# A two-layer vision tower on one core: seven token tiles as split float32r products, ternary weights made on ScalarE, narrower bias products, an epsilon folded into the norm's aggregation, and new instruction orders

## Chip, cores and metric

The kernel runs on one core of one Trainium2 chip. The metric is the device time of one execution in microseconds, as the median of three runs.

## What is computed

The input is 32 images of 3x96x96. They are cut into 36 patches each, so there are 32 x 37 = 1184 tokens of width 256, the first of each image being a class token.

```python
h = tok(x)                            # patches (1152 x 768) @ W.T (768 x 256) + b, class token, + pos_enc
h = h + attn0(_layernorm(h), ...)     # second layernorm, z = sigmoid(n @ Wg.T + bg), c = n @ Wc.T + bc, a scan
                                      # h = (1 - z) h + z c over the tokens of an image, plus its own input
h = h + ffn0(_layernorm(h), ...)      # gelu(x @ absmean(W_fc).T), layernorm(1024) * ln_w + ln_b, @ absmean(W_proj).T
h = h + attn1(_layernorm(h), ...)     # rope, causal softmax attention inside an image, output projection
h = h + ffn1(_layernorm(h), ...)      # round(x / scale) clipped to +-127, @ (ternary - 1).T, + bias

def _absmean_core(W):                 # the ternary weights of ffn0
    gamma = jnp.mean(jnp.abs(W)) + EPS
    Ws = W / gamma
    Wq = jnp.sign(Ws) * jnp.minimum(jnp.round(jnp.abs(Ws)), 1.0)
```

## The kernel before

The 1152 patch rows are 9 tiles of 128. The class tokens are the same for all images up to the attention, so they are carried as one column beside the tiles (stages `c_...`). Each engine has its own program, written out by hand as a string in `ORDER`: `tok:3` is stage `tok` on tile 3, and an engine runs its stages strictly in that order. Semaphores join the engines.

Stages of a tile: **tok** (PE, L661: six products of 128x128 by 128x256 in plain float32, then one for position and bias at L666), copied out of PSUM by ScalarE (`h0`, L925); statistics on VectorE (`stats`, L1093, and `mean`, L1101, a `bn_aggr`); the power -1/2 on GpSimd (`power`, L1540, after `scaled`, L1535, has added epsilon; `shift`, L1544, makes the bias of the normalisation); `n0` normalises (VectorE); **t0** turns the tile on PE (L673); ScalarE writes the high part and VectorE the low part (`low_part`, L1106), since the gate products are sums of three float32r products (hi hi, hi lo, lo hi; `split_product`, L537). **gate** runs over chunks of three tiles, four blocks each, and is read by two sigmoids on ScalarE (L979, L981) and by VectorE's `gate` (L1360); then **scan** (L1382) and `h1`. After that come `n1`, `t1`, `fc`, gelu, `square`, `gw` (L1414), `high` (L1021), `low`, two DMA transposes, `proj`, then `n2`, `t2`, `qk`, `value`, `rope`, `score`, `attend`, and at last `n3`, `t3`, `out`.

PSUM: `NARROW` gives two banks in turn to everything that is listed for it (`tok`, `c_sum`, `c_square`, `h1`, `proj` and others), `WIDE` three banks to `gate`, `fc` and `qk`. A stage that claims a bank waits until the reader of the bank's last owner is done (`drained`). For `tok:2` that is ScalarE's `h0:1`, for `tok:5` it is `h0:3`.

The ternary weights are made by VectorE in two steps for each of two matrices of 128x2048: `w_below` (L1208) and `w_ternary` (L1214), after ScalarE's sums of absolute values (L886, L891). The bias of `ln_b` through `W_proj` is `w_ln_bias`: 16 products of 128x256 in float16 with a broadcast weight. All loads are issued by SyncE in one queue: x tile 0, the two halves of `w_tok`, small tables, x 1 and 2, `w_gate`, x 3 and 4, `w_fc`, `w_out`, x 5 and 6, `w_pj`, x 7 and 8, then the rest.

## Time and profile before

| | us |
|---|---|
| median of 3 runs | 160.49 |
| lowest, highest | 160.1, 162.58 |
| the profiled execution: its time | 159.69 |
| the profiled execution: span of its instructions | 157.9 |
| share of the span busy: PE, VectorE, ScalarE, GpSimd | 89%, 80%, 61%, 55% |
[...]

The span is 1.8 us shorter than the time of the same execution. All stretches below are given in us from the start of the span. PE is TensorE's matmul, PEld its weight load, DVE VectorE, ACT ScalarE, POOL GpSimd, SPq the queue of SyncE.

### The profile page before, as it was taken

Reading aid. Unit: us, or ns where it says so; the run is one execution under the profiler, and the core shown is the slowest. Engines: PE = TensorE matmul, PEld = TensorE weight load, DVE = VectorE, ACT = ScalarE, POOL = GpSimd, SP = SyncE. Lnnn points to the kernel's source line nnn. Section 1 sums busy time; section 2 is a strip of 40 time slices with the busy share of each in tenths; the row PEclk is TensorE's granted clock in tenths of the full one; section 3 lists DMA queues with packets and bytes.
Section 4 is the critical chain, followed back from the end, with each engine's and each line's share of the span. In section 5 each row is a group of like instructions: output and inputs, shape, how many; then the busy total and the mean of one; then the engine's idle time right before and its main releaser. Section 6 shows DMA issues by size and latency. Waiting matters only on the chain.

```text
span 157.9 us, 3087 instructions
## 1 busy us (share of the span) xinstructions
PE 139.8 (89%) x874; PEld 111.3 (71%) x874; DVE 126.4 (80%) x404; ACT 96.0 (61%) x232; POOL 87.2 (55%) x159
## 2 busy tenths in 40 slices
...
GB/s 163 258 398 425 421 391 238 2 0 0 124 46 0 2 2 2 18 119 133 125 111 104 162 113 108 147 106 149 60 55 0 4 0 0 2 4 0 65 144 103
DMA packets 25621, 17.00 MB, mean 108 GB/s; under 512 B 20069, under 2 KB 23173, under 8 KB 25349
## 3 DMA queue, kind: packets, MB, share of 16 engines
q1 hardware_dynamic: 25605, 16.81, 40.3%
...
HBM read 9.70 MB, written 1.21 MB: 69 GB/s over the span
## 4 chain that ended last, share of the span: by engine, by line
DVE 26%; PE 22%; POOL 21%; issue 11%; ACT 8%; DMA 6%; SPq 4%; DVEq 0%; POOLq 0%; ACTq 0%
POOL small L1540 8%; DMA w_out_int<-w_out_in 6%; PE bank L661 5%; SPq L463 4%; POOL keys L1619 4%; POOL small L1535 4%; PE bank L758 3%; DVE stats L1093 3%; DVE gw L1414 3%; DVE gl L1106 2%; PE bank L832 2%; PE bank L792 2%; DVE rope L1460 2%; POOL small L1544 2%; POOL residual L1592 2%
## 5 line engine op out<-in xcount | busy, mean ns | idle before, releaser
L1540 POOL TENSOR_TENSOR small<-small,powers 128x1 f32<-128x1 f32 (+4 forms) x48 | 39.7, 826 | 6.0 <-DVE small L1403 2.8
L661 PE MATMUL bank<-w_tok,x_raw 128*128 128x256 f32 x108 | 27.7, 411 | 5.8 <-DMA w_tok<-w_tok_in 5.6
L661 PEld LDWEIGHTS bank<-w_tok,x_raw 128*128 128x128 f32 x108 | 21.5, 206 | 8.8 <-issue 5.6
L1535 POOL TENSOR_SCALAR small<-small 128x1 f32<-128x1 f32 x36 | 9.4, 260 | 24.9 <-DVE small L1101 23.2
L537 PE MATMUL bank<-pj,gt_hi 128*128 128x256 f16 x72 | 16.2, 273 | 0.7 <-issue 0.7
L537 PE MATMUL bank<-pj,gt_lo 128*128 128x256 f16 x72 | 16.2, 273 | 0.0
L932 ACT ACTIVATE n<-residual,small 128x256 f32<-128x256 f32 x18 | 10.7, 595 | 9.0 <-POOL small L1544 9.0
L537 PE MATMUL bank<-fc,n1t_hi 128*128 128x512 f16 x36 | 13.6, 379 | 0.6 <-ACT g L1002 0.3
L537 PE MATMUL bank<-fc,n1t_lo 128*128 128x512 f16 x36 | 13.6, 379 | 0.0
L1460 DVE SCALAR_TENSOR_TENSOR rope<-bank,packed,consts 128x324 f32<-128x324 f32 (+2 forms) x24 | 13.1, 608 | 0.3 <-POOL query L1613 0.2
L932 ACT ACTIVATE s<-end,small 108x256 f32<-108x256 f32 (+2 forms) x12 | 7.2, 596 | 9.4 <-POOL small L1544 6.2
L673 PE MATMUL bank<-consts,n 128*128 128x128 f32 x54 | 10.5, 281 | 2.6 <-ACT n L932 2.5
L925 ACT ACTIVATE h<-bank 128x256 f32<-128x256 f32 x9 | 3.4, 381 | 15.0 <-PE bank L666 14.9
L1544 POOL TENSOR_SCALAR small<-small 128x1 f32<-128x1 f32 (+3 forms) x30 | 10.5, 351 | 3.0
L1106 DVE TENSOR_TENSOR gl<-gw,gh 128x1024 f16<-128x1024 f32 x9 | 11.0, 1222 | 1.3 <-ACT gh L1021 1.2
L1562 POOL TENSOR_TENSOR cls<-cls,powers 128x1 f32<-128x1 f32 (+1 forms) x4 | 3.3, 832 | 15.7 <-DVE cls L1256 14.8
L1414 DVE SCALAR_TENSOR_TENSOR gw<-g,small,ln_w 128x1024 f32<-128x1024 f32 x9 | 11.5, 1276 | 0.0
L1002 ACT ACTIVATE g<-bank 128x512 f32<-128x512 f32 x18 | 10.6, 590 | 0.2 <-PE bank L537 0.2
L1021 ACT ACTIVATE gh<-gw 128x1024 f16<-128x1024 f32 x9 | 9.5, 1050 | 1.6 <-DVE gw L1414 1.6
L673 PEld LDWEIGHTS bank<-consts,n 128*128 128x128 f32 x54 | 6.7, 144 | 5.3 <-ACT n L932 3.8
L1012 ACT ACTIVATE squares<-g,small 128x1024 f16<-128x1024 f32 x9 | 10.3, 1146 | 0.0
L537 PE MATMUL bank<-n2t_hi,wq_hi 128*128 128x326 f32 (+2 forms) x24 | 9.1, 378 | 0.0
...
## 6 DMA issues: line engine op xcount, KB each, us to landing
...
w_gate<-w_gate_in SPq DMA_DIRECT2D x1, 512.0 KB, 7.3
w_qk<-w_qk_in SPq DMA_DIRECT2D x1, 512.0 KB, 12.5
ln_w<-ln_w_in SPq DMA_DIRECT2D x1, 512.0 KB, 3.6
```

The source lines that it names most:

```text
L537: last = mm(out, a, b, start=(n == 0), stop=(n == len(pairs) - 1))
L661: mm(out[:, 0:D], x_raw[:, i, k, :], w_tok[:, k, :], start=(k == 0), stop=False)
L673: last = nc.tensor.transpose(out[:, k * 128:(k + 1) * 128], rows_tile[:, k * 128:(k + 1) * 128], ident)
L932: return go(out, h[0:n, i, :], ACT.Identity, scale=small[0:n, i, factor:factor + 1], bias=small[0:n, i, shift:shift + 1])
L1002: go(g[:, i % 2, h * 512:(h + 1) * 512], banks[WIDE[("fc", u)][0]][:, :], ACT.Gelu, accum_out=small[:, i, GS + h:GS + h + 1]).then_inc(s[" ...
L1012: go(squares[:, :], g[:, i % 2, :], ACT.Square, bias=small[:, i, MVG:MVG + 1], scale=-1.0, accum_out=small[:, i, GQ:GQ + 1]).then_inc(s["s ...
L1106: tt(out, full, hi, ALU.subtract).then_inc(ready, 1)
L1414: stt(out=gw[:, i % 2, :], in0=g[:, i % 2, :], scalar=col(i, MVG), in1=ln_w[:, :], op0=ALU.subtract, op1=ALU.mult).then_inc(s["gw_ready"], 1)
L1460: last = stt(out=rope[:, t, 0:width].rearrange("p (m t) -> p m t", t=PATCHES), in0=banks[WIDE[("qk", 4 * c + b)][0]][:, first:first + widt ...
L1535: return nc.gpsimd.tensor_scalar(small[0:n, i, out:out + 1], small[0:n, i, value:value + 1], factor, add, ALU.mult, ALU.add)
L1540: return gt(small[0:n, i, r:r + width], small[0:n, i, ve:ve + width], powers[0:n, 0:width], ALU.pow)
L1544: nc.gpsimd.tensor_scalar(small[0:n, i, nb:nb + 1], small[0:n, i, mv:mv + 1], small[0:n, i, r:r + 1], -1.0, ALU.mult, ALU.mult).then_inc(s ...
```

## The change

Five things are changed together.

1. `tok:2` to `tok:8` use split products: `x_hi` (a rounded copy, ScalarE) and `x_lo` (the rest, VectorE, written over `x_raw`), and likewise `wt_hi` and `wt_lo` once for the weights. Each of the six products of a tile becomes three in float32r. `tok:0` and `tok:1` stay plain. `x_hi` has three slots, which lie in the memory of `hs`, so `scan:0` waits for all of `tok`.
2. The ternary weights: ScalarE scales by 1/gamma and adds a large constant that rounds (`w_round`), then takes the sign (`w_sign`). VectorE's `w_below` and `w_ternary` go.
3. `w_ln_bias` becomes `w_ln_col` (the 16 products with `pj` as weights and 2 columns), a reduction on VectorE, and 2 plain products of 128 columns against the identity that spread the column. `c_sum` of 0, 1 and 3 uses one product where it used two, since `c_h0`, `c_h1` and `c_h2` now also write their sum.
4. Norms 1 and 2: the statistics tile has a third group of count 0 whose sum of squares is 256 epsilon, so that the aggregation gives variance plus epsilon, and GpSimd's `scaled` goes there (18 instructions).
5. `ORDER` is new on all four engines.

The diff, cut (orders down to the part with `gate` and `scan`; declarations, semaphore lists and the same edits in `proj` left out):

```diff
     "tensor": """
-        tok:0 c_sum:0 tok:1 w_gate:0 c_square:0 w_gate:1 tok:2 tok:3 w_gate:2 w_gate:3 tok:4 w_ternary:0 t0:0 t0:1
-        tok:5 t0:2 tok:6 t0:3 tok:7 t0:4 gate:0 gate:1 gate:2 t0:5 tok:8 w_value_bias:0 gate:3 w_ln_bias:0 t0:6 t0:7
-        gate:4 h1:0 h1:1 gate:5 h1:2 t0:8 gate:6 gate:7 w_fold:0 gate:8 w_fold:1 c_sum:1 t1:0 gate:9 h1:3 h1:4
...
+        tok:0 c_sum:0 tok:1 w_gate:0 c_square:0 tok:2 tok:3 tok:4 w_gate:1 w_gate:2 tok:5 t0:0 w_ternary:0 t0:1
+        w_gate:3 tok:6 t0:2 tok:7 t0:3 gate:0 t0:4 w_value_bias:0 gate:1 t0:5 gate:2 tok:8 gate:3 w_ln_col:0 t0:6
+        t0:7 w_ln_bias:0 gate:4 gate:5 h1:0 h1:1 gate:6 t0:8 h1:2 w_fold:0 w_fold:1 gate:7 c_sum:1 gate:8 t1:0
...
     "scalar": """
-        w_sel:0 h0:0 h0:1 w_gate:0 h0:2 c_t0:0 w_abs_fc:0 h0:3 w_abs_pj:0 w_abs_ln:0 h0:4 n0:0 n0:1 t0:0 t0:1 n0:2
-        h0:5 t0:2 h0:6 w_ln_b:0 w_qk:0 t0:3 h0:7 t0:4 n0:3 n0:4 gate:0 n0:5 gate:1 h0:8 t0:5 t0:6 t0:7 w_ln_w:0
-        gate:2 t0:8 gate:3 n0:6 w_fold:0 n0:7 n1:0 w_fold:1 t1:0 n1:1 gate:4 gate:5 n1:2 t1:1 fc:0 n1:3 n0:8 t1:2
...
+        w_tok:0 w_sel:0 h0:0 split:2 w_gate:0 split:3 split:4 h0:1 w_abs_fc:0 h0:2 c_t0:0 h0:3 split:5 split:6 h0:4
+        w_abs_pj:0 w_abs_ln:0 split:7 h0:5 split:8 t0:0 w_round:0 t0:1 h0:6 t0:2 w_qk:0 w_sign:0 h0:7 t0:3 w_ln_b:0
+        w_round:1 gate:0 t0:4 w_sign:1 h0:8 t0:5 gate:1 t0:6 n0:0 n0:1 n0:2 t0:7 gate:2 gate:3 t0:8 n0:3 w_fold:0
+        n0:4 n1:0 n0:5 w_fold:1 w_ln_w:0 n1:1 gate:4 t1:0 n0:6 n1:2 gate:5 t1:1 fc:0 fc:1 n0:7 t1:2 fc:2 fc:3 n1:3
...
     "vector": """
-        c_h0:0 w_ones:0 w_pos:0 c_mean:0 c_var:0 w_small:0 stats0:0 mean0:0 stats0:1 stats0:2 c_norm:0 mean0:1
-        c_lo0:0 n0:0 mean0:2 n0:1 w_gate:0 stats0:3 mean0:3 w_gate_bias:0 stats0:4 w_cut:0 n0:2 w_below:0 w_ln:0
-        t0:0 t0:1 n0:3 mean0:4 w_ln_scale:0 stats0:5 w_ternary:0 n0:4 mean0:5 stats0:6 t0:2 w_below:1 n0:5 w_ln_b:0
-        w_qk:0 mean0:6 t0:3 t0:4 w_ternary:1 stats0:7 gate:0 n0:6 scan:0 mean0:7 t0:5 w_value_bias:0 stats0:8 gate:1
-        n0:7 mean0:8 scan:1 w_ln_bias:0 t0:6 n0:8 h1:0 h1:1 t0:7 stats1:0 stats1:1 h1:2 mean1:0 c_h1:0 t0:8 gate:2
...
+        w_ones:0 w_pos:0 c_h0:0 w_tok:0 c_mean:0 stats0:0 split:2 split:3 stats0:1 c_var:0 split:4 mean0:0 mean0:1
+        c_norm:0 w_gate:0 stats0:2 n0:0 stats0:3 n0:1 split:5 mean0:2 w_small:0 stats0:4 split:6 mean0:3 w_cut:0
+        c_lo0:0 stats0:5 n0:2 split:7 w_ln:0 t0:0 split:8 mean0:4 mean0:5 stats0:6 t0:1 t0:2 n0:3 n0:4 w_ln_scale:0
+        w_gate_bias:0 w_qk:0 mean0:6 t0:3 stats0:7 n0:5 mean0:7 n0:6 w_value_bias:0 w_ln_b:0 gate:0 n0:7 scan:0 t0:4
+        stats0:8 w_ln_col:0 mean0:8 t0:5 gate:1 w_ln_bias:0 scan:1 n0:8 t0:6 h1:0 t0:7 h1:1 stats1:0 c_h1:0 stats1:1
+        h1:2 mean1:0 stats1:2 mean1:1 gate:2 w_fold:0 mean1:2 t0:8 scan:2 gate:3 w_fold:1 scan:3 t1:0 c_mean:1
...
     "gpsimd": """
-        w_tok:0 c_pow:0 h0:0 h0:1 h0:2 h0:3 w_ln:0 h0:4 h0:5 h0:6 h0:7 h0:8 h1:0 h1:1 hc:0 hc:1 h1:2 h1:3 hc:2
...
+        w_tok:0 h0:0 c_pow:0 h0:1 h0:2 h0:3 w_ln:0 h0:4 h0:5 h0:6 h0:7 h0:8 h1:0 h1:1 hc:0 h1:2 hc:1 c_pow:1 hc:2
...
+    x_lo = m.at("x_lo", [TILES, KX, TILE], F32R, x_at)
+    x_hi = m.at("x_hi", [X_SLOTS, KX, TILE], F32R, b_at + both)
...
+            def w_ln_col(_i):
+                out = claim(NARROW, ("ln_col", 0))
                 pe.wait_ge(s["pj_ready"], 1)
                 pe.wait_ge(s["ln_b_hi_ready"], 1)
                 pe.wait_ge(s["ln_b_lo_ready"], 1)
-                split_product(out[:, 0:D], [
-                    (part[:, k:k + 1].to_broadcast([128, 128]), pj[:, k, :])
-                    for k in range(KH) for part in (ln_b_hi, ln_b_lo)
-                ]).then_inc(s["pe_ln_bias"], 1)
+                for b in range(KD):
+                    last = split_product(out[:, 2 * b:2 * b + 2], [
+                        (pj[:, k, b * 128:(b + 1) * 128], ln_b_both[:, k, :]) for k in range(KH)])
+                last.then_inc(s["pe_ln_bias"], 1)
+
+            def w_ln_bias(_i):
+                out = claim(NARROW, ("ln_bias", 0))
+                pe.wait_ge(s["ln_bias_ready"], 1)
+                pe.wait_ge(s["dma_consts"], 32)
+                for k in range(KD):
+                    last = mm(out[:, k * 128:(k + 1) * 128],
+                              derived[:, D_LN_COL + k:D_LN_COL + k + 1].to_broadcast([128, 128]), ident,
+                              start=True, stop=True)
+                last.then_inc(s["pe_ln_bias"], 1)
...
-                    columns = range(C_SOURCE[n], C_SOURCE[n] + KD)
-                split_product(out[:, 0:1], [(ones[:, :], cls[:, c:c + 1]) for c in columns])\
+                    column = C_HSUM + n
+                mm(out[:, 0:1], ones[:, :], cls[:, column:column + 1], start=True, stop=True)\
...
             def tok(i):
                 out = claim(NARROW, ("tok", i))
-                pe.wait_ge(dma_x[i], 16)
-                for k in range(KX):
-                    if i == 0 and k % (KX // 2) == 0:
-                        pe.wait_ge(s["dma_w_tok_b" if k else "dma_w_tok"], 16)
-                    mm(out[:, 0:D], x_raw[:, i, k, :], w_tok[:, k, :], start=(k == 0), stop=False)
+                if i < PLAIN:
+                    pe.wait_ge(dma_x[i], 16)
+                    for k in range(KX):
+                        if i == 0 and k % (KX // 2) == 0:
+                            pe.wait_ge(s["dma_w_tok_b" if k else "dma_w_tok"], 16)
+                        mm(out[:, 0:D], x_raw[:, i, k, :], w_tok[:, k, :], start=(k == 0), stop=False)
+                else:
+                    if i == PLAIN:
+                        pe.wait_ge(s["x_hi_ready"], 1)
+                        pe.wait_ge(s["x_lo_ready"], 1)
+                    pe.wait_ge(s["x_hi_ready"], i - PLAIN + 2)
+                    pe.wait_ge(s["x_lo_ready"], i - PLAIN + 2)
+                    for k in range(KX):
+                        hi, lo = x_hi[:, i % X_SLOTS, k, :], x_lo[:, i, k, :]
+                        mm(out[:, 0:D], hi, wt_hi[:, k, :], start=(k == 0), stop=False)
+                        mm(out[:, 0:D], hi, wt_lo[:, k, :], start=False, stop=False)
+                        mm(out[:, 0:D], lo, wt_hi[:, k, :], start=False, stop=False)
...
+            def w_round(n):
+
+                _, w, _ = ternary[n]
+                act.wait_ge(s["cut_ready"], 2)
+                act.wait_ge(s["round_ready"], 2)
+                go(w[:, :, :], w[:, :, :], ACT.Identity, scale=derived[:, D_INV_GAMMA + n:D_INV_GAMMA + n + 1],
+                   bias=derived[:, D_ROUND:D_ROUND + 1]).then_inc(s["rounded_ready"], 1)
+
+            def w_sign(n):
+                out, w, ready = ternary[n]
+                act.wait_ge(s["rounded_ready"], n + 1)
+                go(out[:, :, :], w[:, :, :], ACT.Sign, bias=derived[:, D_ROUND + 1:D_ROUND + 2]).then_inc(s[ready], 1)
...
+            def w_tok_(_i):
+                act.wait_ge(s["dma_w_tok"], 16)
+                act.wait_ge(s["dma_w_tok_b"], 16)
+                go(wt_hi[:, :, :], w_tok[:, :, :], ACT.Copy).then_inc(s["x_hi_ready"], 1)
+
+            def split(i):
+                act.wait_ge(dma_x[i], 16)
+                if i - PLAIN >= X_SLOTS:
+                    act.wait_ge(s["pe_tok"], i - X_SLOTS + 1)
+                go(x_hi[:, i % X_SLOTS, :, :], x_raw[:, i, :, :], ACT.Copy).then_inc(s["x_hi_ready"], 1)
...
                     dve.wait_ge(s[f"stats{norm}_ready"], i + 1)
-                    nc.vector.bn_aggr(col(i, normed[norm][2], 2, n), stats[0:n, norm, i % 2, 0:6])\
+                    if norm in WITH_EPS and i == 0:
+                        dve.wait_ge(s["powers_ready"], 3)
+                    width = 9 if norm in WITH_EPS else 6
+                    nc.vector.bn_aggr(col(i, normed[norm][2], 2, n), stats[0:n, norm, i % 2, 0:width])\
                         .then_inc(s[f"mv{norm}_ready"], 1)
...
+            def w_tok_(_i):
+                dve.wait_ge(s["x_hi_ready"], 1)
+                low_part(wt_lo[:, :, :], w_tok[:, :, :], wt_hi[:, :, :].bitcast(F32), s["x_lo_ready"])
+
+            def split(i):
+                dve.wait_ge(s["x_hi_ready"], i - PLAIN + 2)
+                low_part(x_lo[:, i, :, :], x_raw[:, i, :, :], x_hi[:, i % X_SLOTS, :, :].bitcast(F32), s["x_lo_ready"])
...
-                for sign, c in ((0.5, D_CUT), (-0.5, D_NEG_CUT)):
-                    ts(derived[:, c:c + 2], total, sign / (HID * D), sign * ABS_EPS, ALU.mult, ALU.add)\
-                        .then_inc(s["cut_ready"], 1)
-
-            ternary = ((fc, w_fc, "fc_ready"), (pj, w_pj, "pj_ready"))
-
-            def w_below(n):
-                out, w, _ = ternary[n]
-                dve.wait_ge(s["cut_ready"], 2)
-                ts(out[:, :, :], w[:, :, :], derived[:, D_NEG_CUT + n:D_NEG_CUT + n + 1], None, ALU.is_lt)\
-                    .then_inc(s["below_ready"], 1)
-
-            def w_ternary(n):
-                out, w, ready = ternary[n]
-                dve.wait_ge(s["below_ready"], n + 1)
-                stt(out=out[:, :, :], in0=w[:, :, :], scalar=derived[:, D_CUT + n:D_CUT + n + 1], in1=out[:, :, :],
-                    op0=ALU.is_gt, op1=ALU.subtract).then_inc(s[ready], 1)
+                ts(derived[:, D_GAMMA:D_GAMMA + 2], total, 1.0 / (HID * D), ABS_EPS, ALU.mult, ALU.add)\
+                    .then_inc(s["cut_ready"], 1)
+                dve.wait_ge(s["cut_ready"], 1)
+                nc.vector.reciprocal(derived[:, D_INV_GAMMA:D_INV_GAMMA + 2], derived[:, D_GAMMA:D_GAMMA + 2])\
+                    .then_inc(s["cut_ready"], 1)
+
+            def w_ln_col(_i):
+                dve.wait_ge(s["pe_ln_bias"], 1)
+                nc.vector.tensor_reduce(derived[:, D_LN_COL:D_LN_COL + KD],
+                                        narrow(("ln_col", 0), 128, 2 * KD).rearrange("p (b t) -> p b t", t=2),
+                                        mybir.AxisListType.X, ALU.add).then_inc(s["ln_bias_ready"], 1)
...
+                if n == 0:
+                    dve.wait_ge(s["pe_tok"], TILES)
...
+                nc.gpsimd.memset(stats[:, 1:3, :, 6:8], 0.0).then_inc(s["powers_ready"], 1)
+                nc.gpsimd.memset(stats[:, 1:3, :, 8:9], LN_EPS * D).then_inc(s["powers_ready"], 1)
...
             def h1_(i):
                 pool.wait_ge(s["mv1_ready"], i + 1)
-                scaled(i, VE1, MV1 + 1, 1.0, LN_EPS).then_inc(s["ve1_ready"], 1)
-                pool.wait_ge(s["ve1_ready"], i + 1)
-                power(i, VE1, R1).then_inc(s["r1_ready"], 1)
+                power(i, MV1 + 1, R1).then_inc(s["r1_ready"], 1)
```

## Rows read from the trace of the kernel before

**Rows 1.** Busy time by stretch: from:to, length, engines' busy us (instructions), clock, DMA.
```profile
10.00:20.00 10.00, 9.87 (x52) 8.77 (x51) 3.15 (x17) 2.37 (x5) 1.08 (x3) 1.00 1.03 422
20.00:34.00 14.00, 13.85 (x77) 12.26 (x75) 12.64 (x47) 9.39 (x22) 7.35 (x18) 1.00 0.45 170
...
47.00:62.00 15.00, 14.42 (x85) 11.78 (x83) 14.18 (x46) 11.22 (x25) 8.35 (x18) 1.00 0.01 2
62.00:80.00 18.00, 15.08 (x119) 9.54 (x120) 17.56 (x52) 17.59 (x42) 13.22 (x19) 1.00 0.55 96
93.00:109.00 16.00, 14.31 (x109) 12.28 (x107) 14.77 (x35) 10.58 (x23) 14.43 (x21) 1.00 0.72 127
```

**Rows 2.** Timeline of PE: start us, us; two plain token tiles.
```profile
25.64 2.76 PE L661 MATMUL bank<-w_tok,x_raw 128*128 128x256 f32 x12
28.05 0.47 PE L666 MATMUL bank<-pos,sel 128*128 128x256 f32 x1
```

**Rows 3.** Timeline of PE: first and last of five float32r products, 256 columns.
```profile
87.20 0.28 PE L537 MATMUL bank<-wv_lo,n2t_hi 128*128 128x256 f32 x1
...
87.66 0.28 PE L537 MATMUL bank<-wv_hi,n2t_lo 128*128 128x256 f32 x1
```

**Rows 4.** Timeline of PE: the bias products (first, what follows 16), 16 narrow ones.
```profile
42.45 0.28 PE L537 MATMUL bank<-pj,ln_b_hi 128*128 128x256 f16 x1
...
44.21 0.83 PE L673 MATMUL bank<-consts,n 128*128 128x128 f32 x4
...
65.03 0.54 PE L613 MATMUL bank<-cls_n,fc 128*128 128x2 f16 x16
```

**Rows 5.** Groups by line and form: busy us, mean ns | idle before.
```profile
L1214 DVE SCALAR_TENSOR_TENSOR pj<-w_pj,derived,pj 128x2048 f16<-128x2048 f32 x1 | 2.3, 2342 | 0.0
L1208 DVE TENSOR_SCALAR pj<-w_pj,derived 128x2048 f16<-128x2048 f32 x1 | 1.3, 1275 | 0.0
L1106 DVE TENSOR_TENSOR wq_lo<-w_qk,wq_hi 128x1024 fp32r<-128x1024 f32 x1 | 1.2, 1219 | 0.0
L878 ACT ACTIVATE wq_hi<-w_qk 128x1024 fp32r<-128x1024 f32 x1 | 1.0, 1047 | 0.0
L886 ACT ACTIVATE fc<-w_fc 128x2048 f16<-128x2048 f32 x1 | 1.9, 1894 | 0.0
```

**Rows 6.** Timeline of ScalarE: `h0:1`, the two `w_gate` copies, the sigmoid's table load.
```profile
14.71 0.38 ACT L925 ACTIVATE h<-bank 128x256 f32<-128x256 f32 x1 [3.07 <-PE bank L666]
14.99 1.32 ACT L857 ACTIVATE wg_hi<-w_gate,packed 128x512 fp32r<-128x512 f32 x2
...
36.07 1.28 ACT L979 ACT_TABLE_LOAD   x1
```

**Rows 7.** DMA issues, KB each, us to landing; then the issue in SyncE's timeline.
```profile
w_gate<-w_gate_in SPq DMA_DIRECT2D x1, 512.0 KB, 7.3
...
5.45 0.43 SPq L463 DMA_DIRECT2D w_gate<-w_gate_in  x1
```

**Rows 8.** Timeline of PE: `tok:2`, `gate:0` and `gate:3` start.
```profile
15.55 0.68 PE L661 MATMUL bank<-w_tok,x_raw 128*128 128x256 f32 x2
...
34.35 0.42 PE L537 MATMUL bank<-n0t_hi,wg_hi 128*128 128x386 f32 x1
...
41.21 0.53 PE L537 MATMUL bank<-n0t_hi,wg_hi 128*128 128x386 f32 x1
```

**Rows 9.** Timeline of VectorE: `gate:0`; `gate:2`; the subtraction `low`.
```profile
40.09 0.60 DVE L1360 SCALAR_TENSOR_TENSOR zc<-bank,derived,z 128x386 f32<-128x386 f32 x1
...
49.65 0.61 DVE L1360 SCALAR_TENSOR_TENSOR zc<-bank,derived,z 128x384 f32<-128x384 f32 x1
...
76.01 1.21 DVE L1106 TENSOR_TENSOR gl<-gw,gh 128x1024 f16<-128x1024 f32 x1
```

**Rows 10.** Timeline of GpSimd: `scaled` and `power` for one tile; the same power later.
```profile
49.44 0.19 POOL L1535 TENSOR_SCALAR small<-small 128x1 f32<-128x1 f32 x1 [2.79 <-DVE small L1101]
49.72 0.56 POOL L1540 TENSOR_TENSOR small<-small,powers 128x1 f32<-128x1 f32 x1
...
75.97 1.66 POOL L1540 TENSOR_TENSOR small<-small,powers 128x1 f32<-128x1 f32 x1
```

More of the change, by code:

```diff
@@ L35 @@
 CHUNK_TILES = (3, 3, 3)
+PLAIN = 2
+X_SLOTS = 3
 CHUNKS = len(CHUNK_TILES)
@@ L206 @@
     "w_ternary": lambda i: [("abs_sum", 0)],
+    "w_ln_col": lambda i: [("ln_col", 0)],
     "w_ln_bias": lambda i: [("ln_bias", 0)],
@@ L347, in tower @@
     out_shift = m.at("out_shift", [D], F32R, b_at + both)
+    x_hi = m.at("x_hi", [X_SLOTS, KX, TILE], F32R, b_at + both)
+    assert X_SLOTS * KX * TILE * 4 <= both
     pos_in = m.at("pos_in", [D], F32, b_at)
@@ L574, in w_ternary @@
                     .then_inc(s["pe_abs_sum"], 1)
-            def w_ln_bias(_i):
-                out = claim(NARROW, ("ln_bias", 0))
+            def w_ln_col(_i):
+                out = claim(NARROW, ("ln_col", 0))
                 pe.wait_ge(s["pj_ready"], 1)
@@ L1057, in t3 @@
                     .then_inc(s["q3t_ready"], 1)
-            stages = {"w_sel": w_sel, "w_gate": w_gate_, "w_qk": w_qk_, "w_fold": w_fold,
-                      "w_abs_fc": w_abs_fc, "w_abs_pj": w_abs_pj, "c_t0": c_t0, "c_gelu": c_gelu, "c_t2": c_t2, "w_out_shift": w_out_shift,
+            stages = {"w_tok": w_tok_, "split": split, "w_sel": w_sel, "w_gate": w_gate_, "w_qk": w_qk_, "w_fold": w_fold,
+                      "w_abs_fc": w_abs_fc, "w_abs_pj": w_abs_pj, "w_round": w_round, "w_sign": w_sign, "c_t0": c_t0, "c_gelu": c_gelu, "c_t2": c_t2, "w_out_shift": w_out_shift,
                       "c_value": c_value, "h0": h0_, "n0": n0_, "t0": t0, "gate": gate,
@@ L1235, in c_h0 @@
                 dve.wait_ge(s["dma_packed"], 16)
-                tt(mine(C_H0, KD), packed[:, CLASS:CLASS + KD], packed[:, PLACE:PLACE + KD], ALU.add)\
+                stt(out=mine(C_H0, KD), in0=packed[:, CLASS:CLASS + KD], scalar=1.0, in1=packed[:, PLACE:PLACE + KD],
+                    op0=ALU.mult, op1=ALU.add, accum_out=mine(C_HSUM))\
                     .then_inc(s["cls_vector"], 1)
@@ L1290, in c_h1 @@
                 dve.wait_ge(s["cls_vector"], cls_step("vector", "res0"))
-                tt(mine(C_H1, KD), mine(C_RES0, KD), zc[:, :, 0], ALU.add).then_inc(s["cls_vector"], 1)
+                stt(out=mine(C_H1, KD), in0=mine(C_RES0, KD), scalar=1.0, in1=zc[:, :, 0], op0=ALU.mult, op1=ALU.add,
+                    accum_out=mine(C_HSUM + 1)).then_inc(s["cls_vector"], 1)
             def c_u(_i):
```

132 lines of the change are left out of this document (67 added, 65 removed).

## The prediction

> **What bounds the kernel now.** I read the busy time by stretch first. From 10 to 34 us PE is busy for 23.7 of 24 us, and VectorE, idle for most of the time up to 20 (3.15 of 10), is busy for 12.6 of 14 after that. From 47 to 62 both are full (14.4 and 14.2 of 15), from 62 to 80 VectorE and ScalarE (17.6 each of 18), and from 93 to 109 VectorE and GpSimd (14.8 and 14.4 of 16) [rows 1]. So up to 62 us a gain needs PE and VectorE to come forward together, and behind that less PE work buys nothing. I then read the timelines of PE, ScalarE and VectorE around the token tiles and the gates, for what each of the new orders would wait on [rows 6, 8, 9], and GpSimd's for the norms [rows 10].
>
> **Change, part by part.**
>
> *Split products.* A plain tile takes 28.05 - 25.64 = 2.41 us for its six products [rows 2]. float32r products of 256 columns start (87.66 - 87.20) / 4 = 0.115 us apart [rows 3], so 18 take 2.07. That is 0.34 a tile and 2.4 us for seven, all on PE. In exchange ScalarE copies 768 columns for each tile and 1536 once: the line through 1.05 us at 1024 and 1.89 at 2048 gives 0.84 and 1.47, 7.3 in all. VectorE subtracts as much: 1.22 us at 1024 gives 0.91 and 1.83 in proportion, 8.2 in all [rows 5].
>
> *Ternary weights.* VectorE loses 2 x (1.28 + 2.34) = 7.2 us, and ScalarE gains 4 x 1.89 = 7.6 [rows 5]. So VectorE has 1 us more to do in total than before, and gains only in place: some 4.5 us of the subtractions (weights, tiles 2 to 4) fall into its idle time ahead of 20 us, and the 7.2 us were all behind it. ScalarE gets 15 us more by 41 us, where it has room (2.4 busy of 10, 9.4 of 14) [rows 1], but the second sign stands behind `gate:0` in its queue, and `w_ln_col` on PE waits for it, with `gate:4` behind.
>
> *Narrow bias.* The 16 products take 44.21 - 42.45 = 1.76 us; 16 of 2 columns take at most 0.54 [rows 4]. I add 0.3 for the two products that spread the column (each is two passes of 128 columns): 0.9 saved at least. Three dropped sums are worth another 0.3. `w_ln_bias` now waits for VectorE's reduction; `t0:6` and `t0:7` are put between and cover it. PE's total: 2.4 + 0.9 + 0.3 = 3.6 us.
>
> *What of this passes, by the new orders.* `tok:2` claims the bank that ScalarE's `h0:1` frees. `h0:1` began at 14.71 [rows 6]; now `split:2`, `w_gate`, `split:3` and `split:4` stand ahead of it. `w_gate` can't start before its load lands at 5.45 + 7.3 = 12.75 [rows 7]; with 1.32 [rows 6] and twice 0.84, `h0:1` starts at 15.7 and `tok:2` near 16.0, against 15.55 [rows 8]. Three tiles at 2.25 (2.07 and the position product) and two parts of the gate bias then bring PE to 23.2. `tok:5` needs VectorE's `split:5`. Ahead of that is `c_norm`, which waits for a power on GpSimd that has been put behind the one of tile 0: the statistics of tile 0 come out of VectorE near 17.5, GpSimd needs some 2 us for both, and the 14 instructions from `c_norm` to `split:5` at the mean of 12.64 / 47 = 0.27 [rows 1] and 0.91 for the split end near 24.2. PE idles for 1 us. `tok:5` starts near 24.2, against 25.64 [rows 2]. With three tiles, the turns and a wait for `n0:3`, `gate:0` starts near 32.8, against 34.35 [rows 8]: 1.5 ahead of the 3 that its products alone would give. `t0:5` stands ahead of `gate:2` now and waits for `n0:5`, which VectorE reaches near 36.7, behind `w_qk` (1.22) [rows 5]. So `gate:2` ends near 38.0, `gate:3` starts near 41, hardly ahead of 41.21 [rows 8], while VectorE's own `gate:0`, which needs `gate:2`, comes at 38.2 against 40.09 [rows 9]. `scan:0` waits for `tok:8`, near 40.3. VectorE then runs through the chunk, and I put its `gate:2` (49.65) [rows 9] 1.2 to 1.9 us earlier: 1.6. The bounds for this step: 0 (one more wait like the two above) and 3.6 (all of PE's saving passes).
>
> *Epsilon in the aggregation.* GpSimd's `scaled` and the hop behind it take 49.72 - 49.44 = 0.28 us [rows 10], 18 times: 5.0 us of its work, and 0.28 of every chain from statistics to `n1` or `n2`. GpSimd is close to full only from 93 to 109 [rows 1], where four of the 18 lie. I take these four and one hop for each of the two phases ahead: 1.7 less 0.3, because the `power` behind may then fall under a VectorE instruction that holds it. Taken: 1.4, bounds 0 and 5.0. The wider aggregation reads three more numbers; I price it at nothing, since its neighbours' cost is nearly all fixed.
>
> GpSimd's price is not steady: one power took 0.56 us at 49.72 and 1.66 at 75.97, with VectorE's subtraction of two SBUF operands running from 76.01 to 77.22 [rows 9, 10]. The splits are subtractions of two SBUF operands too. [...]
>
> *Orders behind 62 us.* No work goes there but the sums and epsilon. Moves of `value`, `t3` and `clip` can give or take a us; I take 0.3 as gain from the sums of the class token, which now wait for one product instead of two.
>
> **Sum.** 1.6 + 1.4 + 0.3 = 3.3 us off the profiled execution's 159.69 (span 157.9, and 1.8 around it), which gives 156.4. That execution lies 0.8 below the median of the runs, 160.49, so I predict 157.2, 2.1% less.
>
> **Rivals.**
> - *Forecast* (part of the gain lost to waits on ScalarE and VectorE): 155.7 to 158.7. Chance 0.40.
> - *The saving passes whole*: landings or copies come sooner than I put them, so that neither `h0:1` nor `split:5` holds PE: 3.6, and of epsilon 2.4 since GpSimd's chain sets 93 to 109: 160.49 - 6.0 = 154.5. For it: PE is gapless up to 62 [rows 1]. Against: the order of ScalarE ahead of `h0:1`. Chance 0.24.
> - *No change*: VectorE does as much as before, and is full from 47 to 80; what PE saves turns into waits for it, and epsilon hides behind VectorE: 159 to 161.5. For it: VectorE is 1 us heavier in total [rows 5]. Against: the place of that work. Chance 0.18.
> - *Slower: ScalarE's function tables.* One load is 1.28 us [rows 6]. If the sign is not in the set that is loaded at first nor in the sigmoid's, there are three more loads: before `w_sign:0`, before `w_sign:1` and back for `gate:1`, 3.84 us, all between 32 and 42 us, where PE's `w_ln_col`, `gate:4` and the scans stand behind ScalarE. That takes back the 3.3 and 0.5 more: 161.0, and more with every wait that `gate:1` passes on; two loads (2.56) would leave it below the time before. It decides from 3.3 us on. Against: four other simple functions (copy, identity, absolute value, square) need no load of their own here. Chance 0.18. [...]
>
> **How the numbers follow.** A measurement of this kernel tells about 2% from no change: below 157.3 is faster, above 163.7 slower. Faster: a little over half of the forecast (0.22) and the whole saving (0.24), 0.46. Slower: the upper part of the table rival, with waits behind it, 0.12. The rest, 0.42, is within 2%. The range goes from 153.9, which leaves out the end of the second case, to 161.8, which leaves out most of the slower one.
>
> **What would show each step.** Right: 18 products of a split tile start about 0.115 us apart; `tok:2` starts near 16 and `tok:5` near 24, after an idle PE; `gate:0` of PE near 33; VectorE's `gate:2` near 48; four table loads in all; norm chains of `n1` and `n2` shorter by 0.28. Wrong: float32r pairs further apart than 0.134, where a split tile costs as much as a plain one; more than four table loads; GpSimd's powers in 20 to 30 us longer than before; VectorE's `gate:2` not before 49.6, and then nothing but epsilon is left; or a new wait behind 110 us, where I have only read the old order.

## The result and the profile after

| series | before, median | after, median | ratio, 95% interval |
|---|---|---|---|
| first | 161.39 us (160.1 to 162.58, 4 runs) | 154.91 us (154.44 to 158.13, 4 runs) | 0.961 [0.950, 0.973] |
| second | 159.69 us (158.26 to 161.27, 19 runs) | 155.64 us (154.67 to 158.01, 4 runs) | 0.974 [0.965, 0.983] |
| third | 160.04 us (158.49 to 162.12, 11 runs) | 155.69 us (154.44 to 157.66, 6 runs) | 0.973 [0.966, 0.980] |

Executions more than 1.5% above the fastest of their kernel (in the second and third series those of before at 161.10 to 162.12 us and mean clocks of 0.966 to 0.977, where its others have 0.976 to 0.999) are in the medians, but not in the ratios, nor in the means below, whose number of executions stands in brackets. The change makes the kernel faster, by 6.5 us in the first and smallest series and by 4.0 to 4.4 in the two larger ones. The prediction was 157.2, that is 3.3 us less. The profiled execution of the first series ran at a mean clock of 0.946, the lowest of all executions of this kernel here, so the profile read below is one of the second series: 156.32 us, span 154.5, mean clock 0.976 (the profiled execution of before has 0.978).

The busy time of each engine by stretch, in that profile (from:to, length, then busy us and instructions of PE, PEld, DVE, ACT and POOL, the granted clock, the DMA share and GB/s), answers to [rows 1]:

```profile
10.00:20.00 10.00, 8.16 (x44) 7.12 (x43) 6.64 (x18) 6.30 (x9) 1.67 (x4) 0.87 1.03 420
20.00:34.00 14.00, 13.91 (x117) 13.71 (x117) 11.73 (x45) 11.28 (x22) 6.35 (x16) 0.97 0.47 181
47.00:62.00 15.00, 14.14 (x82) 11.29 (x80) 14.38 (x44) 13.46 (x31) 6.87 (x12) 1.00 0.01 2
62.00:80.00 18.00, 14.76 (x110) 8.78 (x109) 17.10 (x49) 15.99 (x37) 10.53 (x16) 0.91 0.54 95
93.00:109.00 16.00, 15.53 (x120) 13.01 (x117) 15.96 (x38) 11.67 (x26) 14.41 (x17) 1.00 0.69 140
```

From 10 to 20 us PE is busy for 1.7 us less than before, most of it idle time (below), and VectorE for 3.5 more: the splits lie there, as forecast. From 93 to 109 us VectorE is without a gap (15.96 of 16; before 14.77), the first sign of a gain that I had not put into the sum. And the clock, 1.00 in every one of these stretches before, is below 1 in three of them. (The profile of before has a fall of its own outside them: 0.83, 0.50 and 0.82 in the three stretches of 2 us from 136 to 142.)

PE around the split tiles (start us, us, what; in brackets the idle time before it and what ended it), for [rows 2, 4, 8]: `tok:2`; a product in its middle; a tile at a clock of 1.00, first, last and position product; `tok:5`; `gate:3`; the 16 narrow bias products and what follows them.

```profile
16.50 0.39 PE L693 MATMUL bank<-wt_hi,x_hi 128*128 128x256 f32 x1 [1.35 <-ACT h L985]
...
18.28 0.41 PE L695 MATMUL bank<-wt_hi,x_lo 128*128 128x256 f32 x1
18.50 0.41 PE L693 MATMUL bank<-wt_hi,x_hi 128*128 128x256 f32 x1
...
22.62 0.28 PE L693 MATMUL bank<-wt_hi,x_hi 128*128 128x256 f32 x1
...
24.62 0.28 PE L695 MATMUL bank<-wt_hi,x_lo 128*128 128x256 f32 x1
24.73 0.28 PE L700 MATMUL bank<-pos,sel 128*128 128x256 f32 x1
...
25.66 0.37 PE L693 MATMUL bank<-wt_hi,x_hi 128*128 128x256 f32 x1
...
41.29 0.34 PE L549 MATMUL bank<-n0t_hi,wg_hi 128*128 128x386 f32 x1
...
42.62 0.54 PE L549 MATMUL bank<-ln_b_both,pj 128*128 128x2 f16 x16
43.02 0.64 PE L707 MATMUL bank<-consts,n 128*128 128x128 f32 x4
```

A split tile takes 24.73 - 22.62 = 2.11 us for 18 products, where a plain one took 2.41. The 16 bias products take 0.40 instead of 1.76. PE idles for 1.35 us in front of `tok:2`, and then its products start 0.22 us apart (18.28, 18.50) instead of 0.117, at a granted clock of 0.50. In slices of 0.2 us the clock of this profile is 1.00 or 0.50, but for five slices (0.57 to 0.94), each of them between slices of the one and of the other; so a value between the two in a longer stretch comes from a part at 1.00 and a part at 0.50. The same profile in stretches of 2 us, same columns:

```profile
16.00:18.00 2.00, 1.50 (x10) 1.50 (x11) 1.96 (x7) 0.65 (x3) 0.00 (x0) 0.86 1.00 400
18.00:20.00 2.00, 2.00 (x12) 2.00 (x11) 0.06 (x1) 1.81 (x2) 1.67 (x4) 0.50 1.06 431
20.00:22.00 2.00, 2.00 (x15) 2.00 (x15) 1.87 (x5) 0.48 (x2) 1.75 (x4) 0.79 0.97 403
```

ScalarE's `h0:1`, its load of the sigmoid's functions and the second sign, from the timelines of the same profile ([rows 6]), then VectorE's `gate:0` and `gate:2` ([rows 9]):

```profile
16.09 0.36 ACT L985 ACTIVATE h<-bank 128x256 f32<-128x256 f32 x1
...
38.01 1.28 ACT L1039 ACT_TABLE_LOAD   x1
39.30 0.58 ACT L1039 ACTIVATE z<-bank,derived 128x386 f32<-128x386 f32 x1
...
40.51 2.01 ACT L941 ACTIVATE pj<-w_pj,derived 128x2048 f16<-128x2048 f32 x1
42.41 0.39 ACT L985 ACTIVATE h<-bank 128x256 f32<-128x256 f32 x1
...
40.02 0.62 DVE L1429 SCALAR_TENSOR_TENSOR zc<-bank,derived,z 128x386 f32<-128x386 f32 x1 [1.21 <-ACT z L1039]
...
49.56 0.58 DVE L1429 SCALAR_TENSOR_TENSOR zc<-bank,derived,z 128x384 f32<-128x384 f32 x1
```

The sign (L941) runs behind a sigmoid with no load around it. VectorE's `gate:2` is only 0.1 us earlier than before (49.65), yet this execution is 3.4 us faster than the profiled one of before (156.32 against 159.69): next to nothing of its gain comes from the start, and nearly all from what follows.

### The profile page after: what moved, and what is told of

Read it like the earlier page. It is cut to its first block, busy times and chain, and to the rows that moved or that the text cites. A ratio compares the mean times of both kernels' runs of the same rounds, so it can differ in the third digit from the quotient of the medians.

```text
span 156.2 us, 3185 instructions
## 1 busy us (share of the span) xinstructions
PE 139.6 (89%) x914; PEld 111.4 (71%) x914; DVE 128.8 (82%) x414; ACT 110.0 (70%) x244; POOL 79.5 (51%) x143
## 4 chain that ended last, share of the span: by engine, by line
PE 25%; DVE 23%; ACT 16%; POOL 13%; issue 12%; DMA 5%; SPq 3%; DVEq 0%; POOLq 0%
PE bank L549 7%; DMA w_gate<-w_gate_in 5%; DVE rope L1531 4%; POOL small L1610 4%; POOL keys L1687 4%; PE bank L792 3%; DVE gl L1169 3%; SPq L475 3%; POOL residual L1662 3%; DVE stats L1153 2%; PE bank L843 2%; PE bank L866 2%; POOL small L1614 2%; PE bank L693 2%; ACT x_hi L981 2%
## 5 line engine op out<-in xcount | busy, mean ns | idle before, releaser
L1610 POOL TENSOR_TENSOR small<-small,powers 128x1 f32<-128x1 f32 (+4 forms) x48 | 32.0, 669 | 17.4 <-DVE small L1164 11.5
L1605 POOL TENSOR_SCALAR small<-small 128x1 f32<-128x1 f32 x18 | 4.2, 233 | 28.3 <-DVE small L1164 27.3
L549 PE MATMUL bank<-pj,gt_lo 128*128 128x256 f16 x72 | 17.6, 287 | 0.0
L1614 POOL TENSOR_SCALAR small<-small 128x1 f32<-128x1 f32 (+3 forms) x30 | 14.2, 473 | 3.0
L693 PE MATMUL bank<-wt_hi,x_hi 128*128 128x256 f32 x42 | 12.9, 307 | 1.8 <-ACT h L985 1.8
L684 PE MATMUL bank<-w_tok,x_raw 128*128 128x256 f32 x24 | 7.9, 497 | 5.3 <-DMA w_tok<-w_tok_in 5.0
L694 PE MATMUL bank<-wt_lo,x_hi 128*128 128x256 f32 x42 | 12.4, 295 | 0.0
L695 PE MATMUL bank<-wt_hi,x_lo 128*128 128x256 f32 x42 | 12.4, 294 | 0.0
L684 PEld LDWEIGHTS bank<-w_tok,x_raw 128*128 128x128 f32 x24 | 6.0, 258 | 6.5 <-issue 5.0
L693 PEld LDWEIGHTS bank<-wt_hi,x_hi 128*128 128x128 f32 x42 | 8.7, 207 | 1.9 <-ACT h L985 1.9
```

The lines of the kernel that those rows point to most:

```text
L549: last = mm(out, a, b, start=(n == 0), stop=(n == len(pairs) - 1))
L684: mm(out[:, 0:D], x_raw[:, i, k, :], w_tok[:, k, :], start=(k == 0), stop=False)
L693: mm(out[:, 0:D], hi, wt_hi[:, k, :], start=(k == 0), stop=False)
L694: mm(out[:, 0:D], hi, wt_lo[:, k, :], start=False, stop=False)
L695: mm(out[:, 0:D], lo, wt_hi[:, k, :], start=False, stop=False)
L1610: return gt(small[0:n, i, r:r + width], small[0:n, i, ve:ve + width], powers[0:n, 0:width], ALU.pow)
```

## Experiments

The theories: **A**, what the forecast lacks comes from the epsilon, which I had at 1.4 of a possible 5.0 us; **B**, it comes from the new orders behind 62 us, which I had at next to nothing. Beside them stands the question why the start gave so little of PE's 3.6 us. Where means of different series are compared, the changed kernel is at 155.3 in both the second and the third.

**The changed kernel again.** No edit.

> The changed kernel once more, for a profile at an even clock beside runs of before on the same chip. Both theories (A: the gain beyond the forecast comes from the epsilon of the middle norms and the early phase; B: it comes from the new orders behind 62 us) expect 154.5 to 155.5 us, ratio about 0.96. In the profile: VectorE's gate:2 between 47.5 and 48.5 if the start phase gave what was forecast (1.6 us), near 46 if it gave all of PE's 3.6 us, behind 49 if it gave nothing.

155.3 us (3), profile above. `gate:2` at 49.56 says that in this execution the start gave nothing.

**Epsilon alone, on the kernel before, and the change without it.**

```diff
 # eps_only, against before
-    scaled(i, VE1, MV1 + 1, 1.0, LN_EPS).then_inc(s["ve1_ready"], 1)
-    pool.wait_ge(s["ve1_ready"], i + 1)
-    power(i, VE1, R1).then_inc(s["r1_ready"], 1)
+    power(i, MV1 + 1, R1).then_inc(s["r1_ready"], 1)
...
 # no_eps, against after: the same lines back, for norms 1 and 2
```

> The kernel before with one part of the change: the epsilon of the norms n1 and n2 comes into the aggregation as a third group of the statistics, and GpSimd's 18 scaled instructions are gone; all orders are those of before. Theory A: the chains of 93 to 109 us and GpSimd's load pass on 3 us or more of its 5.0: ratio 0.98 or less, 157 to 158 us. Theory B: 1.4 us or less, as in the forecast: ratio 0.991 or more, near 159.5.

> The changed kernel with the epsilon of n1 and n2 back on GpSimd as 18 instructions of their own. Theory A: 3 us or more are lost, 158 or more, ratio to before 0.98 or more. Theory B: 1.4 us or less lost, 156.3, ratio 0.97.

Epsilon alone: 158.5 (7) against 159.4 (17) before, ratio 0.994 [0.989, 0.999]. Taken out of the change: 156.2 (4) against 155.3 (3). Both ways it is worth 0.9 us, though the interval of the first reaches from 0.1 to 1.7 us and the second, of so few executions, isn't clear of noise by itself. That is far from the 3 us or more of A, which falls. The wider aggregation takes 186 ns in the mean (18 of them) where that of two groups takes 170 (9), as these groups of VectorE in the changed kernel show (busy us, mean ns | idle before):

```profile
L1164 DVE BATCH_NORM_AGGREGATE small<-stats 128x2 f32<-128x9 f32 x18 | 3.4, 186 | 0.1
...
L1164 DVE BATCH_NORM_AGGREGATE small<-stats 128x2 f32<-128x6 f32 x9 | 1.4, 170 | 0.0
```

**The order of before, behind 62 us and behind 100 us.**

```diff
 # tail_old: these stages in the relative order of before
 tensor: all behind fc:3 | scalar: behind fc:3 | vector: behind gw:0 | gpsimd: behind h1:3
 # tail_late
 tensor: all behind t2:3 | scalar: behind high:7 | vector: behind gw:8 | gpsimd: behind hc:8
```

> The changed kernel, with the order of before on TensorE and ScalarE behind fc:3, on VectorE behind gw:0 and on GpSimd behind h1:3, which is everything behind about 62 us. Theory A: the new orders there are worth 0.3 us, so 155 to 155.8, ratio 0.965. Theory B: they carry what the forecast lacked, so 157.5 to 158.5, ratio 0.98.

> The changed kernel, but with the relative order of before only behind VectorE's last gw, that is behind about 100 us (the class token's group 0 keeps its new places). With the order of before from 62 us on, the kernel took 157.9 against 155.0 to 155.6. If what the new orders give is earned between 62 and 100 us (in the two profiles VectorE reaches its first rope 52.8 us behind its third gate, against 53.6): within 0.7 of the changed kernel. If it is earned at the end, in clip, round and the last norms: 1.5 to 2.5 us slower than the changed kernel.

The old order from 62 us on: 157.4 (7), 2.0 us more than the changed kernel in the same series. B holds. The old order from 100 us on: 156.5 (5) against 155.3 (4), 1.2 more. That would put about 0.8 us of the 2.0 between 62 and 100 us, and 1.2 behind; neither of the two expectations of the last run was right. Each of these differences is known only to some 1 to 1.7 us, so the total is clear of noise, and the split into two parts is not. The profiles show a place for each. The first is `low:7` on VectorE. Its last three float16 steps (`gw` and `gl`) in the kernel before, with 1.23 us in which VectorE waits for ScalarE's half of `gw:7`:

```profile
97.32 1.27 DVE L1414 SCALAR_TENSOR_TENSOR gw<-g,small,ln_w 128x1024 f32<-128x1024 f32 x1
101.34 1.22 DVE L1106 TENSOR_TENSOR gl<-gw,gh 128x1024 f16<-128x1024 f32 x1 [1.23 <-ACT gh L1021]
102.72 1.28 DVE L1414 SCALAR_TENSOR_TENSOR gw<-g,small,ln_w 128x1024 f32<-128x1024 f32 x1
```

With the old order and all else changed (`tail_old`) the wait is still there, of 0.79 us, first below; in the changed kernel `gw:8` stands ahead of `low:7` and fills it, second below, and so it does in `tail_late`. The 0.8 us from the times are of the size of this wait.

```profile
99.34 1.23 DVE L1169 TENSOR_TENSOR gl<-gw,gh 128x1024 f16<-128x1024 f32 x1 [0.79 <-ACT gh L1081]
```

```profile
99.98 1.26 DVE L1485 SCALAR_TENSOR_TENSOR gw<-g,small,ln_w 128x1024 f32<-128x1024 f32 x1
101.17 0.18 DVE L1164 BATCH_NORM_AGGREGATE small<-stats 128x2 f32<-128x9 f32 x1
101.28 1.17 DVE L1169 TENSOR_TENSOR gl<-gw,gh 128x1024 f16<-128x1024 f32 x1
```

The second is PE in front of the last scores. First the kernel before, whose wait of 1.09 us for GpSimd's keys both old-order variants also have; then the changed kernel:

```profile
134.59 0.68 PE L809 MATMUL bank<-value,pt 109*108 109x256 f32 x2 [0.44 <-DVE end L1492]
136.36 0.98 PE L792 MATMUL bank<-keys,query 128*108 128x109 f32 x8 [1.09 <-POOL keys L1625]
```

```profile
133.37 0.65 PE L843 MATMUL bank<-value,pt 109*108 109x256 f32 x2 [0.31 <-DVE end L1563]
134.53 1.88 PE L826 MATMUL bank<-keys,query 128*108 128x109 f32 x16 [0.50 <-POOL keys L1693]
```

In front of the two rows PE waits for 0.81 us in the changed kernel and for 1.28 in the variant with the old order behind 100 us (0.19 and 1.09): 0.5 of the 1.2 us. I saw the rest in no single wait, and no run changes only one of the two places, so that these waits are the cause is read from the traces and not tested.

**All tiles plain.** Against the changed kernel: `PLAIN = TILES`, and no `split` and no `w_tok` on ScalarE and VectorE.

> The changed kernel with all nine token tiles as plain float32 products, as before; the copies and subtractions for the split (7.3 us of ScalarE, 8.2 of VectorE) are left out too, all else as changed. Forecast of the start phase: PE has 2.4 us more to do, but neither h0:1 nor tok:5 waits for a copy (1.8 and 1.0 us of idle PE): 0.5 us slower than the changed kernel. If the split passes its PE saving on whole: 2.4 us slower, 157.3. If the split tiles give nothing: within 0.3 of the changed kernel, or faster.

156.5 (4), 2.6 us under before in that series (159.05, 5), where the changed kernel lies 4.1 under it in the second and 4.2 in the third. So the splits are worth about 1.6 us, or 1.2 by the plain difference to 155.3; no series has both kernels. That is between the two expected values of 0.5 and 2.4. VectorE's `gate:2` in this profile, at a clock of 1.00 up to there:

```profile
48.88 0.58 DVE L1428 SCALAR_TENSOR_TENSOR zc<-bank,derived,z 128x384 f32<-128x384 f32 x1
```

With the splits and an even clock it is at 48.08 (shown further down): of the 2.4 us that they save on PE, 0.8 have arrived there, and the waits of the start hold the rest.

**Ternary weights on VectorE, with the splits.**

```diff
-    go(w, w, ACT.Identity, scale=INV_GAMMA, bias=ROUND); go(out, w, ACT.Sign, bias=-ROUND)
+    ts(out, w, INV_GAMMA, None, ALU.is_lt); stt(out, w, GAMMA, out, op0=ALU.is_gt, op1=ALU.subtract)
```

> The changed kernel with the ternary weights made on VectorE as before, two instructions of 1.28 and 2.34 us for each matrix in the places of the order before, and nothing of them on ScalarE. If VectorE bounds 20 to 62 us, its 7.2 us more appear nearly whole: 160 to 162. If PE bounds up to 40 us and VectorE has slack by 1 to 3 us there: 157 to 159. If the move to ScalarE is worth nothing: 155.

162.9 (2), ratio to before 1.024 [1.013, 1.035]: 7.6 us slower than the changed kernel of the other series, and slower than before. VectorE's timeline and PE's waits for it, in this kernel:

```profile
34.08 2.34 DVE L1287 SCALAR_TENSOR_TENSOR fc<-w_fc,derived,fc 128x2048 f16<-128x2048 f32 x1
...
40.53 2.35 DVE L1287 SCALAR_TENSOR_TENSOR pj<-w_pj,derived,pj 128x2048 f16<-128x2048 f32 x1
...
36.98 0.58 PE L707 MATMUL bank<-consts,n 128*128 128x128 f32 x2 [2.75 <-DVE n L1420]
44.16 0.45 PE L707 MATMUL bank<-consts,n 128*128 128x128 f32 x2 [1.90 <-DVE n L1420]
```

The 7.2 us arrive nearly whole, as the first expectation has it (its 160 to 162 was a little low), and PE waits for VectorE. VectorE's `gate:2` is at 55.97 here, 6.4 us later than in the changed kernel's profile. The two executions ran at mean clocks of 0.964 and 0.973, where the changed kernel's have 0.978 in the mean of the second and of the third series, so a part of the 7.6 may be the clock. With the ternary weights on VectorE these splits cost more than they save. The move by itself is in the variant of plain tiles: its 2.6 us are no more than the 0.9 of epsilon and the 2.0 of the orders behind 62 us, so the move and the narrow bias alone show no gain. The two parts pay together.

**The two waits of the start.**

```diff
 # h01_early: ScalarE
-w_gate:0 split:3 split:4 h0:1
+w_gate:0 h0:1 split:3 split:4
 # h01_cpow: besides, GpSimd
-h0:0 c_pow:0
+c_pow:0 h0:0
 # and VectorE
-split:2 split:3 stats0:1 c_var:0 split:4 mean0:0 mean0:1 c_norm:0
+split:2 stats0:1 c_var:0 split:3 mean0:0 mean0:1 split:4 c_norm:0
```

> The changed kernel with ScalarE's h0:1 right behind the copy of the gate's weights, ahead of split:3 and split:4. tok:2 on PE should start 1.5 us sooner, as h0:1 stands 1.7 us sooner. If PE's idle time in front of tok:2 passes to the end: 153.5. If tok:5 waits for VectorE's split:5 all the same (its place hangs on c_norm, not on tok:2), the new idle time is in front of tok:5 and the end hardly moves: 154.5 to 155.2.

> As the kernel with h0:1 early, and with the class token's first norm brought forward on both engines that it uses: c_pow:0 ahead of h0:0 on GpSimd, stats0:1, c_var:0 and the first two aggregations ahead of split:3 or split:4 on VectorE, so that c_norm and with it split:5 come sooner. If both waits of PE (in front of tok:2 and of tok:5) are what keeps the start phase from passing its 3.6 us: 1.5 to 2.5 us faster than the changed kernel, 152.5 to 153.5. If VectorE's own work from 24 to 47 us bounds: as the changed kernel, within 0.5.

> The kernel with h0:1 and the class token's first norm early, once more beside the changed kernel. If PE's idle time in front of tok:2 costs through the granted clock (1.35 us idle, then about 5 us at the lower level in the changed kernel's profile, and VectorE's third gate at 49.6 instead of 48.1 us): 1 us or more faster than the changed kernel, 154 or less. If that fall of the clock is rare or costs nothing: within 0.5.

With `h0:1` early, PE does not idle in front of `tok:2`, 0.29 us in front of `tok:4` (first row), and 1.26 us in front of `tok:5`, which waits for `split:5` behind `c_norm`:

```profile
19.83 0.38 PE L693 MATMUL bank<-wt_hi,x_hi 128*128 128x256 f32 x1 [0.29 <-ACT h L985]
24.36 0.36 PE L693 MATMUL bank<-wt_hi,x_hi 128*128 128x256 f32 x1 [1.26 <-DVE x_lo L1169]
```

The idle time moved into the next wait, as expected: `gate:2` is at 48.11, where `tail_late`, with the same wait in front of `tok:2` as the changed kernel and an even clock, has it at 48.08. The time was 156.8 (4), above the 154.5 to 155.2 that were expected, with an interval (ratio 0.985 [0.979, 0.992]) that just touches that of the changed kernel; its profiled execution, 155.72, ends no later than that one's, and why the other three were slower I can't say.

With the class token's norm early as well, 153.7 (3) and, in the next series, 154.1 (5) against 155.3 (4) of the changed kernel there: 1.2 us faster, known to about 1 us. VectorE in the second of these profiles, `c_norm` and `split:5`, and then `gate:2`:

```profile
17.30 0.22 DVE L1330 TENSOR_SCALAR cls<-cls 128x2 f32<-128x2 f32 x1
...
21.42 0.95 DVE L1169 TENSOR_TENSOR x_lo<-x_raw,x_hi 128x768 fp32r<-128x768 f32 x1
...
46.81 0.58 DVE L1429 SCALAR_TENSOR_TENSOR zc<-bank,derived,z 128x384 f32<-128x384 f32 x1
```

`split:5` comes 1.8 us sooner than with `h0:1` early alone (23.27), PE never waits for it, and `gate:2` is 2.8 us ahead of before: of the 3.6 us that PE saves, most reach the gates, if both waits go. This profile is of the fastest of the six executions, 153.12; of the mean gain of 1.2 us it shows more than there is. Ratio to before 0.969 [0.962, 0.976].

**The changed kernel, a third series.** No edit; it serves as the measure for the three other runs of that series (`tail_late`, the second of the two above, and the next).

> The changed kernel again, beside the three below on one chip, so that a us can be told: 154.5 to 155.5 us, higher in executions in which the granted clock falls twice.

155.3 (4).

**Work for PE in its idle time near 62 us.**

```diff
 # tensor: "h1:6 warm:0 h1:7"
+def warm(_i):
+    out = claim(WIDE, ("fc", 4))
+    for _ in range(8):
+        mm(out[:, :], n1t_hi[:, 0, 0:TILE], fc[:, 0, 0:512], start=True, stop=True)
```

> The same kernel, with eight extra float16 products of 512 columns on PE (some 1.7 us of work that nobody reads, into a bank that the next stage overwrites) behind h1:6, in the place where PE is idle for 1.79 us near 62 us. The profiles of after and of four variants show the granted clock at half from there for 2 to 4 us. If the idle time makes the clock fall and the slower products then delay ScalarE and VectorE: no such fall in 60 to 70 us, and 0.5 to 1.5 us faster than without. If VectorE bounds here whatever the clock does: the same time. If the extra products stand in the way of h1:7: up to 1 us slower.

154.2 (6), the same as without it (154.1, 5). The extra products do fill PE's idle time from 60 to 62 us (busy 0.70 of 2 us without them, 1.94 with them). But the fall of the clock was not removed: both profiles have 0.72 from 66 to 72 us. The one without the extra products first:

```profile
60.00:62.00 2.00, 0.70 (x4) 0.46 (x5) 1.97 (x6) 0.99 (x2) 0.55 (x1) 1.00 0.00 0
66.00:72.00 6.00, 5.85 (x34) 3.85 (x34) 5.47 (x19) 6.00 (x13) 3.93 (x7) 0.72 0.54 102
```

```profile
60.00:62.00 2.00, 1.94 (x11) 0.76 (x9) 2.00 (x5) 0.81 (x2) 0.04 (x1) 1.00 0.00 0
66.00:72.00 6.00, 5.23 (x29) 3.63 (x30) 5.29 (x16) 6.00 (x14) 3.37 (x5) 0.72 0.64 120
```

With the extra products the fall only comes later (0.88 from 66 to 68 us and 0.50 from 68 to 70, where without them 66 to 68 has 0.54). In both, PE idles again just ahead of it, for 0.85 us in front of a turn of `n1` and 0.42 behind that. So the run doesn't tell whether idle time brings the fall; it shows that work in one idle stretch didn't prevent it.

All six executions lie within 153.55 and 154.59, at mean clocks of 0.988 to 0.998, while those of the kernel without the filling go from 153.12 to 155.94 at 0.972 to 0.988. That looks like a steadier kernel, but one profile of each doesn't show how.

## Why the prediction was right, and where it was not

The time lies in the range and the mechanism of the forecast was at work; its terms were not all of the right size. The range, 153.9 to 161.8, held the whole saving as well as no change, so that the time lies in it says little, and the terms are what can be judged.

- *Split products and narrow bias.* 2.11 us for the 18 against 2.07 said, 0.40 for the 16 narrow products against at most 0.54. ScalarE's copies take 835 ns each and 1482 once (said 0.84 and 1.47), VectorE's 949 and 1755 (0.91 and 1.83).
- *The waits of the start.* `h0:1` at 16.09 (said 15.7) and `tok:2` at 16.50 (16.0). The changed kernel's own profile is at a clock of 0.50 behind that, from 18 to 20 us. The variant with the old order behind 100 us has the same start and a clock of 1.00 up to 34 us, so the forecast is read there: PE idles for 1.74 us in front of `tok:2`, `tok:5` starts at 24.34 (24.2), `gate:0` at 32.80 (32.8) and `gate:3` at 39.85 (41). `tok:5` and `gate:0` are within 0.2 us of the forecast, and `gate:3` is 1.2 earlier; of the idle 1 us that I had put in front of `tok:5` only 0.25 is there, as the larger part of the idle time falls in front of `tok:2`.
- *Start phase, 1.6 us.* VectorE's `gate:2` was to be at 48.0. In that same variant it is; first `tok:5` on PE, then `gate:2`:

```profile
24.34 0.36 PE L693 MATMUL bank<-wt_hi,x_hi 128*128 128x256 f32 x1 [0.25 <-DVE x_lo L1169]
...
48.08 0.57 DVE L1429 SCALAR_TENSOR_TENSOR zc<-bank,derived,z 128x384 f32<-128x384 f32 x1
```

  In the changed kernel's own profile it is at 49.56, 1.5 us later, with the fall of the clock between: the three stretches of 2 us from 16 to 22 us (0.86, 0.50, 0.79) add up to some 3.4 us at 0.50, where the products start 0.22 us apart against 0.117. I had forecast the idle time, and not a fall behind it. My sign of a wrong forecast, `gate:2` not before 49.6 "and then nothing but epsilon is left", was met to within 0.04 us, and more than epsilon was left all the same, behind the gates. By the times, before against the old tail (159.4 - 157.4 = 2.0) less the epsilon (0.9) leaves 1.1 for the start and the class sums.
- *Epsilon, 1.4.* It was 0.9, inside its bounds, and its interval of 0.1 to 1.7 us doesn't exclude the 1.4. A mean of 0.9 for 18 hops of 0.28 says that most of them are hidden, as the forecast had it, which counted six.
- *Orders behind 62 us, 0.3 with the class sums.* This is the term that was mis-sized: 2.0 us for the orders. The step that failed is "Moves of `value`, `t3` and `clip` can give or take a us": I read which stages moved, and not in front of which of them an engine stood idle. The wait of 1.23 us at `low:7` and that of 1.09 in front of the last scores were both in the trace of before; the new order fills the first and more than halves the second.
- Together 1.1 + 0.9 + 2.0 = 4.0 us, against 4.1 between the means of the second series; said were 3.3. This sum is no check of the terms: the 1.1 is what is left over, so it has to come out. The splits' own 1.2 to 1.6 us would even be more than all of the start, which shows how far such terms can be trusted, about 1 us each. That the sum missed the gain by only 0.7 to 0.8 us there, with one term at 0.3 instead of 2.0, is owed to the terms for start and epsilon, which stood 0.5 us each above these means: some luck, as far as these means can tell.
- *Rivals.* The saving did not pass whole: the variant without the two waits is 1.2 us faster still. By the time alone it can't be dismissed: its 154.5 is nearer to the three medians than 157.2 is, though its gain of 6.0 us is further from the 4.0 and 4.4 of the two larger series than 3.3 is. What speaks against it are the two waits in the traces. That nothing changes fell with the ratios of all three series. The function tables fell too: there are four loads of 1283 ns, as many as before, though ScalarE now computes signs. The first sign runs at 33.34 with no load since the one at 6.70, the second at 40.51 behind the sigmoid's load at 38.01, with none between; so neither sign brought a load here. The sigmoid begins 0.01 us after its load has ended (38.01 + 1.28, 39.30), and the instruction in front of the load ends 0.02 us before it begins (35.86 + 2.13, 38.01), so the load costs its 1.28 us and next to nothing around it.
- *GpSimd beside the splits.* I had read a power of 1.66 us beside VectorE's subtraction `low`, against 0.56 elsewhere, and the sum has no term for such a price at the splits. In this profile no power of `n0` begins while a subtraction of a split runs; one begins 0.34 us ahead of such a subtraction and takes its usual 0.69 us. So no price was paid, and none was measured. What I overlooked is the other side: in the kernel before, the powers of two `n0` tiles begin 0.08 us behind VectorE's `w_below` and `w_ternary` (33.26 and 33.18, 37.57 and 37.49) and take 1.74 and 2.81 us, and those instructions are gone. (`w_below` takes 1.27 us and reads one tensor of 128x2048, not two, so a long power doesn't stand only beside two of them; what makes it long no run shows.) The nine powers of `n0` take 9.8 us before and 6.8 after. No run tells what these 3.0 us of GpSimd are worth. First before, VectorE and GpSimd, then the changed kernel:

```profile
37.49 2.34 DVE L1214 SCALAR_TENSOR_TENSOR pj<-w_pj,derived,pj 128x2048 f16<-128x2048 f32 x1
37.57 2.81 POOL L1540 TENSOR_TENSOR small<-small,powers 128x2 f32<-128x2 f32 x1
```

```profile
25.83 0.69 POOL L1610 TENSOR_TENSOR small<-small,powers 128x2 f32<-128x2 f32 x1
26.17 0.94 DVE L1169 TENSOR_TENSOR x_lo<-x_raw,x_hi 128x768 fp32r<-128x768 f32 x1
```
